# Five of the six iterations of the landmark inverse, with two matrix products each in place of three

## The reference, cut to what matters

```python
def _iterative_inv(K, n_iter=6):
    I = jnp.eye(K.shape[-1])
    denom = jnp.max(jnp.sum(K, axis=-2), axis=-1)[..., None, None]
    V = K.swapaxes(-1, -2) / denom
    for _ in range(n_iter):
        KV = K @ V
        V = 0.25 * V @ (13.0 * I - KV @ (15.0 * I - KV @ (7.0 * I - KV)))
    return V
...
P = _iterative_inv(softmax(q_l k_l^T))          # one 64x64 matrix for each head
N = softmax(q_l k^T)
y = softmax(q k_l^T) @ (P @ (N @ v))
```

## Time and profile before

| what | value |
|---|---|
| median of 3 executions | 1328.4 us |
| lowest, highest | 1325.68, 1328.64 us |
| the profiled execution, its own time | 1328.34 us |
| span of the profiled execution | 1326.6 us |
| mean granted clock of TensorE | 0.959 of full speed |
| PE, PEld busy | 1222.7 us, 610.7 us |
| DVE, ACT, POOL busy | 1023.2 us, 835.4 us, 260.9 us |

### The profile page before, as it was taken

One profiled execution on the slowest core, in us unless ns is written; L12 is line 12 of the kernel. 1 busy time (PEld: TensorE's weight loads), 2 busy tenths in 40 slices (PEclk: granted clock), 3 DMA queues, 4 the chain that ended last, 5 costly groups with the idle time before them and its releaser, 6 DMA issues. The chain is left out here.

```text
span 1326.6 us, 28720 instructions
## 1 busy us (share of the span) xinstructions
PE 1222.7 (92%) x11329; PEld 610.7 (46%) x11329; DVE 1023.2 (77%) x1736; ACT 835.4 (63%) x1479; POOL 260.9 (20%) x376
## 2 busy tenths in 40 slices
PE   6979999999999999999999978888899799899980
PEld 3652333333233232333323345555799566688870
DVE  5879999999999999999999446665775788433324
ACT  2643888888888888888888845555222466533331
POOL 4200220000100001100001011100573222145560
PEclk9986999999999999999999989998998899999995
DMA  4653022122123221211211122000010211223317
GB/s 143 189 192 76 20 60 62 31 63 51 50 65 71 53 59 42 65 47 46 63 38 72 73 60 72 12 10 17 19 44 28 70 38 35 60 79 102 104 41 193
DMA packets 71762, 86.75 MB, mean 65 GB/s; under 512 B 13876, under 2 KB 45324, under 8 KB 70596
## 3 DMA queue, kind: packets, MB, share of 16 engines
q1 hardware_dynamic: 66540, 74.80, 20.5%
q0 software_dynamic: 5088, 10.12, 2.5%
HBM read 45.91 MB, written 38.56 MB: 64 GB/s over the span
## 5 line engine op out<-in xcount | busy, mean ns | idle before, releaser
L633 DVE TENSOR_REDUCE b_mx<-psum 128x1 f32<-128x512 f32 x1014 | 628.2, 682 | 10.4 <-PE psum L562 8.1
L695 ACT ACTIVATE b_exp_ring<-psum 128x512 f32<-128x512 f32 x1024 | 528.6, 601 | 96.6 <-PE psum L732 96.4
L562 PE MATMUL psum<-b_k,b_q 64*128 64x512 bf16 x1024 | 346.4, 392 | 8.0 <-PEq L226 2.8
L723 PE MATMUL psum<-b_q,b_k 64*128 64x512 bf16 x1024 | 292.5, 381 | 0.0
L732 PE MATMUL psum<-b_qr,b_kr 64*128 64x512 bf16 x1024 | 290.0, 378 | 0.0
L745 PE MATMUL psum<-b_exp_ring,b_v 128*32 128x512 f32 x2048 | 272.7, 605 | 0.7 <-ACT b_exp_ring L695 0.7
L723 PEld LDWEIGHTS psum<-b_q,b_k 64*128 64x128 bf16 x1024 | 72.6, 94 | 215.4 <-ACT b_exp_ring L695 184.5
L562 PEld LDWEIGHTS psum<-b_k,b_q 64*128 64x128 bf16 x1024 | 79.1, 94 | 114.3 <-DVE b_mx L633 79.5
L797 POOL CAST b_neg<-b_neg_all 16x128 bf16<-16x128 f32 x32 | 9.0, 281 | 569.5 <-ACT b_neg_all L683 569.5
L732 PEld LDWEIGHTS psum<-b_qr,b_kr 64*128 64x128 bf16 x1024 | 75.3, 95 | 58.1 <-issue 0.5
L1895 ACT ACTIVATE e_hT<-psum,e_b 128x358 f32<-128x358 f32 (+3 forms) x96 | 53.7, 560 | 75.6 <-PE psum L1915 72.3
(11 more groups left out here) (280 smaller groups left out, 1461.3 us busy)
## 6 DMA issues: line engine op xcount, KB each, us to landing
b_q<-q_ops SPq DMA_DIRECT2D x64, 96.0 KB
b_k<-k_ops SPq DMA_DIRECT2D x64, 96.0 KB
k_ops<-a_k SPq DMA_DIRECT2D x20, 256.0 KB, 3.4
x_disp<-b_zeros SPq DMA_DIRECT2D x13, 320.0 KB
e_x<-x_disp SPq DMA_DIRECT2D x8, 520.0 KB
v_ops<-a_vs SPq DMA_DIRECT2D x4, 1024.0 KB, 5.1
b_v<-v_ops SPq DMA_DIRECT2D x16, 256.0 KB
av_out<-b_acc SPq DMA_DIRECT2D x128, 32.0 KB, 1.7
```

The costliest lines, as they stand in the source:

```text
L562: return g.nc.tensor.matmul(g.bank(n % M_RING), g.q0[c][rows, p, t * P:(t + 1) * P], g.k0[c][rows, p, j % 2 * BANK:(j % 2 + 1) * BANK], st ...
L633: nc.vector.reduce_max(maximum_of(mx, x, j), g.bank(n % M_RING), AX.X).then_inc(sem("b_max_done"), 1)
L695: act.activation(ex[:, n % E_RING, :], g.bank(SB + u % 4), ACT.Exp, scale=ATT_SCALE)\
L723: nc.tensor.matmul(g.bank(SB + i), k[s][rows, p, kb * P:(kb + 1) * P], q[s][rows, p, i // 2 * BANK:(i // 2 + 1) * BANK], start=True, stop= ...
```

## The change

The polynomial is written out as 13 A - 15 A^2 + (7 A - A^2) A^2, with W = [A^2, A z], C = 7 A - A^2 and U = 13 [A z] - 15 W, so that an iteration needs W = A [A z] and C W, both with 72 columns, and U is added. The factor of a quarter is no longer applied in each iteration; what is stored is scaled down by 3.25 for each iteration done (`grown`), and the constants take that up. The sixth iteration keeps its three products (two with 64 columns and the narrow one).

On the engines, for each of the first five iterations: PE has two stages of four groups with 72 columns. ACT copies W from PSUM (576 elements on each partition). DVE makes C (`cubic`, 512 elements, both inputs in SBUF) and U (`rest`, 576 elements, both inputs in SBUF) of each group, then `landmarks`, and then for each group the new `AZ` (`iterated`, 576 elements, one input in PSUM). Ahead of the sixth iteration DVE makes its first factor of `AZ` for each group (`factor`), behind the last `iterated`. POOL's scatters wait for `i_mm` at 8 + t, with 8 groups an iteration.

```diff
-AHEAD = 12
+AHEAD = 8
...
-    PR = 3 * NG
+    PR = 2 * NG
+    LAST = ITERS - 1
+    grown = lambda it: 3.25 ** it
...
-                pool.wait_ge(sem("i_mm"), AHEAD + t * (PR * (ITERS - 1) - AHEAD) // NT)
+                pool.wait_ge(sem("i_mm"), AHEAD + t * (PR * LAST - AHEAD) // NT)
...
+            def cubic(it, n):
+                nc.vector.scalar_tensor_tensor(grp(C, n), grp(AZ, n)[:, :, 0:LM], 7.0 / grown(it),
+                                               grp(W, n)[:, :, 0:LM], ALU.mult, ALU.subtract).then_inc(sem("i_c"), 1)
+
+            def rest(it, n):
+                nc.vector.scalar_tensor_tensor(grp(U, n), grp(W, n), -15.0 * grown(it) / 13.0,
+                                               grp(AZ, n), ALU.mult, ALU.add).then_inc(sem("i_u"), 1)
+
+            def iterated(it, n):
+                nc.vector.scalar_tensor_tensor(grp(AZ, n), pairs_of(n)[:, :, 0:ZW], grown(it) ** 3 / 13.0,
+                                               grp(U, n), ALU.mult, ALU.add).then_inc(sem("i_az"), 1)
+
+            def factor(n, src, i):
+                nc.vector.scalar_tensor_tensor(grp(C, n), src, -grown(LAST), eye(i), ALU.mult, ALU.add)\
+                  .then_inc(sem("i_c"), 1)
...
-                dve.wait_ge(sem("i_a"), n + 1)
-                first(n)
-            for it in range(ITERS):
-                for stage in range(2):
-                    for n in range(NG):
-                        dve.wait_ge(sem("i_mm"), at(it, PR, stage * NG + n + 1))
-                        nc.vector.scalar_tensor_tensor(grp(X, n), squares(2 * n + stage), -1.0, eye(1 + stage),
-                                                       ALU.mult, ALU.add).then_inc(sem("i_x"), 1)
+            for it in range(LAST):
+                for n in range(NG):
+                    dve.wait_ge(sem("i_sq"), NG + at(it, NG, n + 1))
+                    cubic(it, n)
+                    rest(it, n)
                 if it < B:
                     landmarks(it)
-                for n in range(NG if it + 1 < ITERS else 0):
-                    dve.wait_ge(sem("i_az"), at(it, NG, n + 1))
-                    first(n)
+                for n in range(NG):
+                    dve.wait_ge(sem("i_u"), at(it, NG, n + 1))
+                    dve.wait_ge(sem("i_mm"), at(it, PR, NG + n + 1))
+                    iterated(it, n)
+            for n in range(NG):
+                dve.wait_ge(sem("i_az"), at(LAST - 1, NG, n + 1))
+                factor(n, grp(AZ, n)[:, :, 0:LM], 0)
+            for stage in range(2):
+                for n in range(NG):
+                    dve.wait_ge(sem("i_mm"), at(LAST, PR, stage * NG + n + 1))
+                    factor(n, squares(2 * n + stage), 1 + stage)
...
-                    act.wait_ge(sem("i_mm"), at(it, PR, 2 * NG + n + 1))
-                    if it + 1 < ITERS:
-                        act.activation(grp(AZ, n), pairs_of(n)[:, :, 0:ZW], ACT.Copy, scale=0.25).then_inc(sem("i_az"), 1)
...
+                    act.wait_ge(sem("i_mm"), at(it, PR, n + 1))
+                    act.activation(grp(W, n), pairs_of(n)[:, :, 0:ZW], ACT.Copy).then_inc(sem("i_sq"), 1)
...
+            for it in range(LAST):
+                for n in range(NG):
+                    if it == 0:
+                        pe.wait_ge(sem("i_a"), n + 1)
+                    else:
+                        pe.wait_ge(sem("i_az"), at(it - 1, NG, n + 1))
+                    products(n, pairs_of(n)[:, :, 0:ZW], a_of, lambda p, half: AZ[half, p, :], "i_mm")
+                for n in range(NG):
+                    pe.wait_ge(sem("i_c"), at(it, NG, n + 1))
+                    products(n, pairs_of(n)[:, :, 0:ZW], c_of, lambda p, half: W[half, p, :], "i_mm")
```

More of the change, by code:

```diff
@@ L1491, in _ @@
                 act.wait_ge(sem("i_kt_ps"), n + 1)
-                act.activation(grp(X, n), squares(4 + n), ACT.Copy).then_inc(sem("i_kt"), 1)
-            for it in range(ITERS):
+                act.activation(grp(W, n)[:, :, 0:LM], squares(4 + n), ACT.Copy).then_inc(sem("i_sq"), 1)
+            for it in range(LAST):
                 for n in range(NG):
-                    act.wait_ge(sem("i_mm"), at(it, PR, 2 * NG + n + 1))
-                    if it + 1 < ITERS:
-                        act.activation(grp(AZ, n), pairs_of(n)[:, :, 0:ZW], ACT.Copy, scale=0.25).then_inc(sem("i_az"), 1)
-                    else:
-                        act.activation(grp(z, n), pairs_of(n)[:, :, LM:ZW], ACT.Copy, scale=0.25).then_inc(sem("i_az"), 1)
+                    act.wait_ge(sem("i_mm"), at(it, PR, n + 1))
+                    act.activation(grp(W, n), pairs_of(n)[:, :, 0:ZW], ACT.Copy).then_inc(sem("i_sq"), 1)
+            for n in range(NG):
+                act.wait_ge(sem("i_mm"), at(LAST, PR, 2 * NG + n + 1))
+                act.activation(grp(z, n), pairs_of(n)[:, :, LM:ZW], ACT.Copy, scale=0.25 * grown(LAST))\
+                   .then_inc(sem("i_az"), 1)
             act.wait_ge(sem("i_wm_clear"), 1)
@@ L1515, in _ @@
             k_of = lambda p, half: g.KS[half, p, :]
-            x_of = lambda p, half: X[half, p, :]
+            c_of = lambda p, half: C[half, p, :]
+            w_of = lambda p, half: W[half, p, 0:LM]
             a_of = lambda p, half: AZ[half, p, 0:LM]
@@ L1526, in _ @@
                   .then_inc(sem("i_colsum"), 1)
-            pe.wait_ge(sem("i_kt"), NG)
+            pe.wait_ge(sem("i_sq"), NG)
             for n in range(NG):
-                products(n, squares(4 + n), x_of, x_of, "i_gram")
+                products(n, squares(4 + n), w_of, w_of, "i_gram")
             pe.wait_ge(sem("i_z0"), 1)
-            for it in range(ITERS):
-                for stage in range(2):
-                    for n in range(NG):
-                        pe.wait_ge(sem("i_x"), at(it, PR, stage * NG + n + 1))
-                        products(n, squares(2 * n + stage), a_of, x_of, "i_mm")
-                cols = slice(LM if it + 1 == ITERS else 0, ZW)
-                for n in range(NG):
-                    pe.wait_ge(sem("i_x"), at(it, PR, 2 * NG + n + 1))
-                    products(n, pairs_of(n)[:, :, cols], x_of, lambda p, half: AZ[half, p, cols], "i_mm")
+            for it in range(LAST):
+                for n in range(NG):
+                    if it == 0:
[6 more added lines that the diff above has]
+                    products(n, pairs_of(n)[:, :, 0:ZW], c_of, lambda p, half: W[half, p, :], "i_mm")
+            for stage in range(2):
+                for n in range(NG):
+                    pe.wait_ge(sem("i_c"), at(LAST, NG, stage * NG + n + 1))
+                    products(n, squares(2 * n + stage), a_of, c_of, "i_mm")
             for n in range(NG):
-                pe.wait_ge(sem("i_az"), at(ITERS - 1, NG, n + 1))
+                pe.wait_ge(sem("i_c"), at(LAST, NG, 2 * NG + n + 1))
+                products(n, pairs_of(n)[:, :, LM:ZW], c_of, lambda p, half: AZ[half, p, LM:ZW], "i_mm")
+            for n in range(NG):
+                pe.wait_ge(sem("i_az"), at(LAST, NG, n + 1))
                 products(n, narrow(2 * n + 1), k_of, lambda p, half: z[half, p, :], "i_landmark")
```

11 lines of the change are left out of this document (5 added, 6 removed).

## The result

| | before | after |
|---|---|---|
| median, executions | 1328.52 us, 4 | 1317.97 us, 4 |
| lowest, highest | 1325.68, 1329.42 | 1316.18, 1319.58 |
| the profiled execution, its span | 1328.34, 1326.6 | 1316.18, 1314.5 |
| mean granted clock of TensorE | 0.959 | 0.955 |
| PE, DVE, POOL busy | 1222.7, 1023.2, 260.9 | 1207.6, 1024.7, 262.1 |

The changed kernel is faster: the medians are 10.6 us apart, and the ratio is 0.9928 [0.9916, 0.9940], which is 9.6 us [8.0, 11.2]. The forecast was a gain of 14.2 us, so a quarter to a third of it is missing. That part is what the rest of this text looks for.

The account below looks back on a forecast made before the run. PE's chain was taken to bound the block. PE's side 14.8 us earlier (1012.6), POOL level at 1012.7, and 0.6 for two level engines gave a gain of 14.2: 1328.34 to 1314 us, range 1311.5 to 1319.5.

Parts of the forecast that it names:

- The price of PE: In each of five iterations, 8 groups of 72 columns at 1.00 us: 8.00 in place of 11.46, 3.46 less each.
- DVE's queue: In an iteration, `cubic` 0.60 and `rest` or `iterated` 0.67 from start to start, `landmarks` 0.34: 8.1 us in all.
- Rival C: DVE sets the pace by full durations or added waits: 9.2 us an iteration, gain 9.2, 1319.1 us; chance 0.10.
- Rival E: Slower: DVE's operations with two SBUF inputs take contended time in every iteration, 15.2 us each, 1347 us; chance 0.03.
- F: No change: every one of POOL's 32 scatters takes 1.72 us, landed at 1024.4, gain 3, 1325.3 us; chance 0.02.
- D: The clock falls early, as the narrow stage starts: 2.9 us more, a gain of 11.9, 1316.4 us; chance 0.10.
- landed 1 us later at 1012.7: End of POOL's scatters: ending at 1011.7, landed 1 us later, level with PE's side done at 1012.6.
- The 16.5 us of reserve: At the end of the block before the change, POOL stands about 16.5 us behind PE's chain (1027.4 less 1010.9).
- the 0.6 that had been allowed for two level engines: At the block's end, PE and POOL being level, the later comes out 0.6 us behind either: 1013.2, gain 14.2.
- rival B: POOL's scatters end last, stretched to 1.72 us each beside DVE's operations: landed 1016.2, gain 11.2, 1317.1 us; chance 0.12.
- The sign of being wrong that was named: At the meeting: the prediction is wrong if the meeting waits for POOL at 1016 or later.
- 3 x 8.15: Iterations 2 to 4 in the sum on PE's chain: 8.15 us each, just over PE's 8.00.

Follow-up runs that it names:

- gpsimd_late: The changed kernel with all of POOL's work in the block (counting, fills, scatters) held back until the five iterations are over; 1366.4 us, one execution.
- no_rest: The changed kernel without `rest`, `iterated` adding the old `AZ` in its place, so the result is no inverse; 1312.4 us, one execution.
- fills_late: The changed kernel with POOL's settings of `f_spread` and `f_sums` moved behind its scatters; 1315.21 us, ratio 0.9914.
- fills_ahead: The changed kernel with POOL's settings of `w_landmark`, `f_spread` and `f_sums` moved into the block before; 1313.46 us, ratio 0.9894.
- filled_stall: The changed kernel with 32 extra, unused PE products of 56 columns in the stall ahead of the sixth iteration; 1316.17 us, ratio 0.9912.
- before_with_stall: The kernel before, with seven unused DVE additions ahead of the sixth iteration's first factor, so that PE stands idle there; 1334.60 us, ratio 1.0042.
- wide_tail: Settings moved into the block before, plus narrow stage and products with z computed on 72 columns in place of 8, against the changed kernel; 1313.34 us, ratio 0.9895.
- folded: The changed kernel with two products in all six iterations, POOL's settings ahead, 15 folded into the factor and no `rest`; 1309.73 us, ratio 0.9865.
- all_six: The changed kernel with two products in the sixth iteration as well; 1317.48 us, ratio 0.9921.
- factor_early: The changed kernel with each `factor` put right behind its group's `iterated` in iteration 5; 1317.86 us, ratio 0.9922.
- folded_wide: The folded kernel with its sixth iteration's second product and the products with z made 72 columns wide; 1309.85 us, ratio 0.9861.

## Why the prediction came out as it did

**Right by its own steps.** The price of PE (1.00 us a group of 72 columns) holds in every iteration. So does DVE's queue: `cubic` 0.68 and `rest` 0.75 with starts 0.60 and 0.67 apart, and a chain of 8.15, measured as 8.17 and 8.18. In the table by stretches of the changed kernel, iteration 3 shows what was named as the sign, both engines over 95%:

```profile
966.99:975.16 8.17, 8.17 (x256) 8.07 (x256) 8.16 (x14) 2.60 (x4) 6.08 (x6) 1.00 0.14 45
```

Rival C (9.2 an iteration) is refuted by this row. Rival E (contention in every iteration, slower) is refuted by the 0.68 and 0.75 beside scatters: what slows DVE is POOL's arithmetic and its `affine_select`, not its issues of DMAs. F (every scatter at 1.72) is refuted by the 41.7 us that the 32 took. D's fall at the start of the narrow stage did not come; the clock fell once ahead of it, behind the stall, and again 5.7 us after that stage began. The stall was 2.22 where 2.3 were forecast.

**The terms that were mis-sized.** Counted from the start of the block, so that the 2.46 us ahead of it drop out:

| term | predicted | measured | runs that show it |
|---|---|---|---|
| iteration 1, contention | 1.8 | 2.25 | gpsimd_late, no_rest |
| iteration 2, contention | 0 | 1.1 | fills_late, fills_ahead |
| fall of the clock behind the stall | 0 (bound 2.9) | 1.6 | filled_stall, before_with_stall |
| fall in the products with z | unchanged | 1.3 less | the timeline above |
| PE's side done (the last copies) | 74.1 | 76.2 | |
| POOL's first scatter | 29.9 | 31.3 | no_rest |
| the 32 scatters | 43.3 | 41.7 | |
| from the last issue to POOL's report | 1.0 | 4.3 | all with POOL last |
| POOL reports | 74.2 | 77.3 | |
| the block | 75.3 | 77.8 | |

The prediction's step that failed is "landed 1 us later at 1012.7": it took a landed packet for the end of POOL's work. It was 1.35 to the landing and 2.95 more to the report. The 16.5 us of reserve had the same fault: by the table of reports it was 13.3 us (1027.4 less 1014.08). Its stretching was off both ways (the start 1.4 later than forecast, the scatters 1.6 quicker), which by luck nearly cancels. POOL reports 3.1 us later than forecast, and since it is last, that is the block's loss against the forecast, less the 0.6 that had been allowed for two level engines: 2.5 us, all of it. PE's own errors (0.45 + 1.1 + 1.6 - 1.3, and 0.2 in small ones, 2.1 in all) are real, but in this execution they are hidden behind POOL. They would have cost most of it alone: with PE last, its end at 75.9 and a wait of 0.92 make a block of 76.8, 1.5 over the forecast, and POOL adds the last 1.0. The prediction saw this place as rival B, but with another price: scatters of 1.72 us beside DVE's operations. That didn't happen: 2 of the 32 took 1.54. So 1317.97 stands close to B's 1317.1, and POOL is last as in B, for a reason that is not B's. The sign of being wrong that was named, a meeting that waits for POOL at 1016 or later, was missed narrowly: 77.3 us into a block that began as before would be 1015.8.

The step on the second iteration failed because 8.15 was taken for 2 to 4 alike ("3 x 8.15"), while POOL's settings, which lie at 959.5 to 966.1, fall into iteration 2 of the changed kernel. The four settings of `f_spread` took 2.24 us before and take 3.10 now. A rule of the Trainium skill, GPSIMD Engine Reference, section Key points, says that the contention is with any VectorE instruction with two SBUF inputs; the measurements agree for POOL's arithmetic and for `affine_select`, show it on both sides, and show none on DVE beside the memsets and the scatters. Taken seriously, the rule asked for a price in iteration 2.

**Behind the block** 2.1 us were lost. The first table row is of the changed kernel, the second of the kernel before, each from the start of the next block:

```profile
1014.00:1126.00 112.00, 104.09 (x1120) 70.34 (x1124) 87.42 (x106) 66.35 (x73) 30.68 (x34) 0.89 0.15 44
```

```profile
1028.00:1138.00 110.00, 100.62 (x1116) 68.45 (x1120) 87.28 (x106) 66.25 (x73) 30.85 (x35) 0.94 0.15 45
```

The granted clock is 0.89 there against 0.94: from PE's first product in it to its last with `f_klm`, 25.4 us are at 1.2 GHz and not 13.4, and that stretch lasts 111.0 us and not 108.9. This accounts for the 2.1. Over all thirteen traces the two go together: 13.4 to 13.7 us of low clock in the stretch with 108.9 (before, fills_late, wide_tail), 16.8 and 17.3 with 109.5 and 109.6 (filled_stall, folded), 20.9 to 21.2 with 110.1 (before_with_stall, all_six, factor_early), 23.9 to 25.5 with 110.7 to 111.0 (folded_wide, no_rest, the changed kernel, fills_ahead), 26.2 with 111.4 (gpsimd_late). Why the clock stays low for longer in some of them is open; the change alone isn't it, since fills_late has it too and is as short as before. The profiled execution of the changed kernel is also its quickest, 1.8 us under its median, so that 12.2 us from profile to profile are 10.6 from median to median.

## What to carry to other kernels

An engine off the critical path is in reserve only up to the moment at which it reports at the meeting, not up to its last packet: read the idle time between its last instruction and its first one behind the meeting in a kernel where it comes last, and take that off the reserve. When a change frees the bound engine by more than the reserve, every further gain there is worth nothing until the second engine's work is moved (here 7.5 us of PE's time were worth 0, and moving POOL's settings, which brought its first scatter 6.6 us forward, was worth 3.2 us in the block and 4.5 between the medians). And an operation with two SBUF inputs on DVE is to be priced together with what GpSimd computes beside it, for both engines.

## What the runs showed of the hardware

- GpSimd's report at the meeting came 2.91 to 2.95 us after its last landing, and 2.95 after its last operation on SBUF (fills_late), wherever it came last.
- Contention goes both ways. DVE's operation of 576 elements lasts 0.75 alone and up to 1.83 beside POOL's arithmetic of 512 elements, which itself goes from 1.27 to 1.70; four `affine_select` of 128 elements take 1.52 alone, 2.24 beside DVE before, and 3.10 now. Beside POOL's memsets and its issues of DMAs DVE's operations kept their 0.69 and 0.75.
- The clock: a pause of PE of 2.1 to 2.2 us behind dense work was followed by a fall to 1.2 GHz in three of six profiled executions, 0.6 to 1.5 us after work resumed, for 3.4 us. Pauses of 0.25 to 1.5 us in the block were not followed by one, and neither was a longer one of 2.75 us in iteration 1 of folded and folded_wide.
- At the end of the block, with products of 8 columns (128 in 3.7 us at full clock), the clock fell in the course of 256 of them in all eleven kernels that have them, and the second 128 took 5.3 to 7.0 us. The same products with 72 columns took 4.2 us at full clock in both kernels that have them, and the fall came 2.7 and 1.5 us into the next block.
